# Kernel with wavelet, sparse attention and full attention, eight images, one core: the lone second attention of the last image gets instruction lists of its own

## The reference, cut to what matters

```
q = Wq x + bq ; k = Wk x + bk ; v = Wv x + bv          # 16 rows for q and k, 128 for v
attn = softmax(q^T k * 0.25, over the 4096 keys)
out  = gamma * (Wo (v attn^T) + bo) + x
```

## Time and profile before

| What | us |
|---|---|
| Three runs | 6031.35, 6034.84, 6043.09 |
| Their median | 6034.84 |
| The profiled execution: its span (the profile gives no other time for it) | 6037.8 |
| Last image's lone second attention, first matmul to end of span | 5557.97 to 6037.8, so 479.8 |

### The profile page before, as it was taken

One profiled execution on the slowest core, in us unless ns is written; L12 is line 12 of the kernel. 1 busy time (PEld: TensorE's weight loads), 2 busy tenths in 40 slices (PEclk: granted clock), 3 DMA queues, 4 the chain that ended last, 5 costly groups with the idle time before them and its releaser, 6 DMA issues.

```text
span 6037.8 us, 91146 instructions
## 1 busy us (share of the span) xinstructions
PE 4861.0 (81%) x30180; PEld 3018.9 (50%) x30180; DVE 4690.6 (78%) x8351; ACT 4552.4 (75%) x6907; POOL 429.0 (7%) x133
## 2 busy tenths in 40 slices
PE   4344788887988888887888878887888878886888
PEld 2000356553666446553556546553565535662666
DVE  3777699977998689977899778986898869984443
ACT  2995699948998589957999489966999589983223
POOL 3001200030000300021000300012000300000000
PEclk7555799997999889997999979998999979997999
DMA  1001200012001200012000120012000120011000
GB/s 64 6 10 48 69 14 15 14 53 71 19 15 50 72 16 15 16 55 69 16 15 20 62 58 15 17 56 70 14 15 14 52 71 19 14 36 39 9 11 10
DMA packets 104798, 199.90 MB, mean 33 GB/s; under 512 B 36632, under 2 KB 41656, under 8 KB 100184
## 3 DMA queue, kind: packets, MB, share of 16 engines
q1 hardware_dynamic: 104280, 193.56, 10.4%
HBM read 110.61 MB, written 82.05 MB: 32 GB/s over the span
## 4 chain that ended last, share of the span: by engine, by line
DVE 31%; PE 22%; issue 21%; ACT 18%; POOL 3%; SPq 2%; DMA 2%; DVEq 1%; ACTq 0%; POOLq 0%
ACT work L981 11%; DVE MX L1587 8%; PE PS L540 6%; DVE M L1438 6%; DVE arena L1516 5%; DVE work L1430 3%; PE PS L506 3%; DVE work L1422 3%; DVE work L1398 3%; ACT work L997 3%; POOL RN L2188 3%; ACT work L1004 2%; PE PS L859 2%; PE PS L844 2%; PE PS L756 2%
## 5 line engine op out<-in xcount | busy, mean ns | idle before, releaser
L981 ACT ACTIVATE work<-arena,T 128x1024 bf16<-128x1024 f32 x1792 | 2039.6, 1140 | 75.2 <-DVE T L1385 48.3
L540 PEld LDWEIGHTS PS<-V,work 128*128 128x128 f32 x16384 | 2010.1, 194 | 122.4 <-issue 29.5
L540 PE MATMUL PS<-V,work 128*128 128x129 f32 x16384 | 2040.3, 278 | 22.6 <-ACT work L1004 22.6
L1587 DVE TENSOR_REDUCE MX<-PS 128x1 f32<-128x512 f32 x2048 | 1395.1, 685 | 421.4 <-PE PS L506 403.9
L1004 ACT ACTIVATE work<-PS 128x1024 f32<-128x1024 f32 x1024 | 1040.4, 1016 | 410.9 <-PE PS L524 408.7
L506 PE MATMUL PS<-KP,QP 96*128 96x512 bf16 x2048 | 850.6, 417 | 352.7 <-DVE MX L1587 312.7
L1516 DVE SCALAR_TENSOR_TENSOR arena<-PS,work 128x1024 f32<-128x1024 f32 x512 | 622.5, 1216 | 100.7 <-ACT work L997 99.2
L524 PE MATMUL PS<-QP,KP 99*128 99x512 bf16 x2048 | 621.3, 385 | 69.3 <-ACT work L1004 38.4
L506 PEld LDWEIGHTS PS<-KP,QP 96*128 96x128 bf16 x2048 | 200.6, 98 | 924.2 <-DVE MX L1587 836.0
L997 ACT ACTIVATE work<-PS 128x1024 f32<-128x1024 f32 x512 | 520.3, 1016 | 142.9 <-PE PS L476 142.6
L1438 DVE MAX8 M<-work 128x8 f32<-128x1024 f32 x512 | 623.9, 1220 | 3.3
(11 more groups left out here) (180 smaller groups left out, 3994.4 us busy)
## 6 DMA issues: line engine op xcount, KB each, us to landing
scr<-work SPq DMA_DIRECT2D x96, 256.0 KB
work<-scr SPq DMA_DIRECT2D x128, 192.0 KB, 2.7
work<-in_x SPq DMA_DIRECT2D x16, 1024.0 KB, 7.7
arena<-in_x SPq DMA_DIRECT2D x8, 2048.0 KB, 11.3
scrX<-arena SPq DMA_DIRECT2D x8, 2048.0 KB, 14.1
XR<-scrX SPq DMA_DIRECT2D x64, 256.0 KB, 2.8
out<-YO SPq DMA_DIRECT2D x64, 256.0 KB, 2.1
scrL<-work SPq DMA_DIRECT2D x24, 512.0 KB, 14.8
```

Of the source, the lines that this page charges most:

```text
L540: last = mm(PS[:, 5 + i // 2, 136 * (i % 2):136 * (i % 2) + 129], P1[:, (16 * j + k) % 3, t, 128 * i:128 * i + 128], V1[:, mt, :], start=( ...
L981: A(JKA[:, m % 2, :], scores(h, i), ACT.Sign, scale=-1.0, bias=T[:, h % 2, i:i + 1], accum_out=CA[:, h % 2, i:i + 1]).then_inc(s["ca"], 1)
L1587: V.reduce_max(MX[:, c % 2, i, w:w + 1], PS[:, maxbank(c, k), :], AX.X).then_inc(s["mr"], 1)
```

## The change

Only the call `slots(8, False, True)` gets other instructions. All new banks and waits hang on `both` or `l0`, which is true in the merged stages.

- PSUM: maxima alternate between banks 4 and 7. The pairs of transposed scores alternate between 2, 3 and 0, 1.
- Waits: `maxima(c, k)` waits for the reduce before the last one, `l1_score` for the exponential before the last one. `maxima(c, 0)` waits for one output less. `l1_turn(j)` waits for one MPT more.
- Lists: PE, ACT, DVE and SP walk a list of their own. On PE, scores run up to two steps ahead of the weighing, three maxima lie around the halves of each weigh for k = 1 to 10, and `l1_turn(j - 1)` moves to just before the weigh 14 of chunk j. The first score of chunk j + 1 is put ahead of weigh 15 of chunk j.

```
-        def maxbank(c, k):
+        def maxbank(c, k, both):
+            if not both:
+                return 4 if k % 2 == 0 else 7
             return 6 if c == 0 and k % 2 else 4
+
+        def pairbanks(k, both):
+            return 2 if both or k % 2 == 0 else 0
...
@@ SP, slots
+                if l1 and not l0:
+                    for j in range(-1, NCH + 1):
+                        if chunk(j):
+                            load_rows(a, j)
+                        if chunk(j + 1):
+                            max_rows(a, j + 1)
+                        if chunk(j - 1):
+                            store(a, j - 1)
+                    return
...
@@ PE, maxima
-                    pe.wait_ge(s["mr"], a * 256 + c * 32 + k + (0 if c == 0 and k else 1))
+                    if l0:
+                        pe.wait_ge(s["mr"], a * 256 + c * 32 + k + (0 if c == 0 and k else 1))
+                    elif c or k:
+                        pe.wait_ge(s["mr"], a * 256 + c * 32 + k)
+                    else:
+                        pe.wait_ge(s["mr"], a * 256 + 1)
...
-                        pe.wait_ge(s["y1"], a * NCH + c + 1)
+                        pe.wait_ge(s["y1"], a * NCH + c + (1 if l0 else 0))
...
@@ PE, l1_score
-                    pe.wait_ge(s["e1"], a * 128 + j * 16 + k + 1)
+                    pe.wait_ge(s["e1"], a * 128 + j * 16 + k + (1 if l0 or (j == 0 and k == 0) else 0))
...
-                        last = mm(PS[:, 2 + t, :], KP1[0:KA, 128 * mt:128 * mt + 128], QP1[0:KA, j * 512:j * 512 + 512],
+                        last = mm(PS[:, pairbanks(k, l0) + t, :], KP1[0:KA, 128 * mt:128 * mt + 128], QP1[0:KA, j * 512:j * 512 + 512],
...
@@ PE, l1_weigh(j, k, halves=(0, 1)): one half is 8 of the 16 instructions
-                    for t in range(2):
+                    for t in halves:
...
-                    last.then_inc(s["pv1"], 1)
+                    if halves[-1] == 1:
+                        last.then_inc(s["pv1"], 1)
...
@@ PE, l1_turn
-                    pe.wait_ge(s["mpt"], a * NCH + min(j + 1, NCH - 1) + 2)
+                    pe.wait_ge(s["mpt"], a * NCH + min(j + (1 if l0 else 2), NCH - 1) + 2)
...
+                def chunks():                                  # PE
+                    for j in range(-1, NCH):
+                        l1_score(j, 1)
+                        maxima(j + 1, 0)
+                        maxima(j + 1, 1)
+                        for k in range(14):
+                            if k + 2 < 16:
+                                l1_score(j, k + 2)
+                            if 1 <= k < 11:
+                                maxima(j + 1, 3 * k - 1)
+                            l1_weigh(j, k, (0,))
+                            if 1 <= k < 11:
+                                maxima(j + 1, 3 * k)
+                            l1_weigh(j, k, (1,))
+                            if 1 <= k < 11:
+                                maxima(j + 1, 3 * k + 1)
+                            if k == 12:
+                                maxrow(j + 1)
+                        l1_turn(j - 1)
+                        l1_weigh(j, 14)
+                        l1_score(j + 1, 0)
+                        l1_weigh(j, 15)
...
+                if not l0:
+                    chunks()
+                    l1_turn(NCH - 1)
                     return
...
@@ ACT, l1_exp
-                    A(P1[:, (16 * j + k) % 3, :, :].rearrange("p t n -> p (t n)"), PS[:, 2:4, :].rearrange("p a n -> p (a n)"),
+                    u = pairbanks(k, l0)
+                    A(P1[:, (16 * j + k) % 3, :, :].rearrange("p t n -> p (t n)"), PS[:, u:u + 2, :].rearrange("p a n -> p (a n)"),
...
+                def chunks():                                  # ACT
+                    for j in range(-1, NCH):
+                        for k in range(14):
+                            l1_exp(j, k)
+                        maxrow(j + 1)
+                        l1_exp(j, 14)
+                        l1_exp(j, 15)
...
+                def chunks():                                  # DVE
+                    for j in range(-1, NCH):
+                        l1_norm(j - 1)
+                        maxima(j + 1, 0)
+                        maxima(j + 1, 1)
+                        for k in range(2, 32):
+                            maxima(j + 1, k)
+                        parts(j + 1)
+                        l1_out(j - 1)
+                    l1_norm(NCH - 1)
+                    l1_out(NCH - 1)
```

More of the change, by code:

```diff
@@ L505, in maxima @@
                     i, w = divmod(k, 8)
-                    mm(PS[:, maxbank(c, k), :], QP1[0:KS, c * 512 + 128 * i:c * 512 + 128 * i + 128], KP1[0:KS, 512 * w:512 * w + 512],
+                    mm(PS[:, maxbank(c, k, l0), :], QP1[0:KS, c * 512 + 128 * i:c * 512 + 128 * i + 128], KP1[0:KS, 512 * w:512 * w + 512],
                        start=True, stop=True).then_inc(s["m"], 1)
@@ L520, in l1_score, with l1_weigh @@
                         pe.wait_ge(s["mq"], a * (NCH * 48) + j * 48 + 96)
-                    pe.wait_ge(s["e1"], a * 128 + j * 16 + k + 1)
+                    pe.wait_ge(s["e1"], a * 128 + j * 16 + k + (1 if l0 or (j == 0 and k == 0) else 0))
                     for t in range(2):
                         mt = 2 * k + t
-                        last = mm(PS[:, 2 + t, :], KP1[0:KA, 128 * mt:128 * mt + 128], QP1[0:KA, j * 512:j * 512 + 512],
+                        last = mm(PS[:, pairbanks(k, l0) + t, :], KP1[0:KA, 128 * mt:128 * mt + 128], QP1[0:KA, j * 512:j * 512 + 512],
                                   start=True, stop=True)
                     last.then_inc(s["st1"], 1)
-                def l1_weigh(j, k):
+                def l1_weigh(j, k, halves=(0, 1)):
                     if not chunk(j):
@@ L677, in alone @@
                         score_t(h + 1, 3)
+                def chunks():
[20 more added lines that the diff above has]
+                        l1_weigh(j, 15)
                 if not l1:
                     alone()
+                    return
+                if not l0:
+                    chunks()
+                    l1_turn(NCH - 1)
                     return
@@ L1586, in maxima @@
                     dve.wait_ge(s["m"], a * 256 + c * 32 + k + 1)
-                    V.reduce_max(MX[:, c % 2, i, w:w + 1], PS[:, maxbank(c, k), :], AX.X).then_inc(s["mr"], 1)
+                    V.reduce_max(MX[:, c % 2, i, w:w + 1], PS[:, maxbank(c, k, l0), :], AX.X).then_inc(s["mr"], 1)
                 def parts(c):
@@ L1817, in alone @@
                         count(h + 1, 2, 7)
-                if l1:
+                def chunks():
[9 more added lines that the diff above has]
+                    l1_out(NCH - 1)
+                if l1 and not l0:
+                    chunks()
+                elif l1:
                     for h in range(-1, NH + 1):
```

## The result

| | before | after |
|---|---|---|
| Median of the runs, us | 6033.1 (4 runs, 6030.0 to 6043.1) | 5931.43 (4 runs, 5928.1 to 5939.3) |
| Ratio | | 0.9832, 95% interval 0.9818 to 0.9846 |
| Profiled span, us | 6037.8 | 5928.3 |
| Lone stage, first maxima matmul to end of span | 479.8 | 5549.04 to 5928.3, so 379.3 |
| Chunk 0, from its first score to its norm | 56.2 | 45.3 |

The kernel is 101.7 us faster (1.7%), against 100 forecast. The stage alone gives 100.5 in the two profiles: 6 x 13.80 + 10.9 + 6.8. The other 8.9 us between the two spans lie ahead of the stage, where no instruction was changed. The first maxima matmul of the stage stands at 5557.97 before and at 5549.04 after.

The account below looks back on a forecast made before the run. PE's work plus waits behind one maxima bank and at chunk ends bound the stage; savings of 83 (chunks 1 to 6), 9.8 (chunk 0) and 6.8 us (last), off median 6034.84, gave 5935 us, range 5924 to 5953.

Parts of the forecast that it names:

- A step: PE's score and weigh take 2.22 us, 16 times a chunk; the ten steps with three maxima matmuls take 2.88.
- The switch cost: Switching PE between bf16 and fp32 around weigh halves: taken as 0; exposed weight loads could cost 14 us in 7 chunks.
- A chunk: Norm to norm, chunks 1 to 6: 44.0 us against 57.81, saving 83 us over six.
- The stall at its end: PE's stall during the norm at a chunk's end: 0.3 us instead of 1.5, possibly between 0 and 1.5.
- Chunk 0: First score to last weigh issued: 42.7 us plus 3.5 for the lower clock, 46.2 against 56.0; saved 9.8.
- Last chunk: Norm to norm without maxima: 35.5 + 1.0 + 0.3 = 36.8 us against 43.6; saved 6.8.
- The range: 5924 to 5953 us: unknown costs from -3 to about +14 or +9, run spread -3.5 to +8.
- The clock: PE's granted clock after chunk ends: no more falls expected with the stall cut from 1.5 to 0.3 us.
- 1 (two banks as one): Maxima banks behave as one, three-maxima steps take at least 3.5 us instead of 2.88: 5979 us, chance 0.08.
- 2: Next chunk's first score gets its rows late, or the norm's cover fails: 25 us in seven chunks, 5960, chance 0.06.
- rival 3: PE's clock stays at or swings to the lower level in the new order: 6277 us if throughout, chance 0.03.
- 4: The new list makes no difference, the stage being bound by something the trace doesn't show: 6035 us, chance 0.01.

Follow-up runs that it names:

- e1: Changed kernel with one maxima bank and the wait for the reduce just before, score pairs staying two: 51.08 us a chunk, ratio to before 0.9961.
- e4: Changed kernel's new banks and waits, but the old merged lists on all engines: 46.92 us a chunk, ratio to before 0.9876.
- e3: Changed kernel with the turn back at the chunk's end, output right behind the norm, old waits: 45.91 us a chunk, one 47.54, ratio to before 0.9856.
- e6: Changed kernel with two maxima, then an undivided weigh, then the third maximum: 46.76 us a chunk, ratio to before 0.9869.
- the repeat: The changed kernel run again with nothing altered, beside the other experiments: 44.01 us a chunk, median 5936.73 us, ratio to before 0.9833.
- e2: Changed kernel with one score pair and the wait for the exponential just before, two maxima banks staying: 45.84 us a chunk, ratio to before 0.9862.
- e5: Changed kernel with PE's row of maxima (maxrow) one step later, behind weigh 13 instead of 12: 44.60 us a chunk, ratio to before 0.9845.
- e7: Changed kernel's new lists, but one maxima bank, one score pair and the stricter waits: 52.41 us a chunk, ratio to before 0.9970.

## Why the prediction was right

- **What bounds the stage.** PE's work plus waits behind one maxima bank: e1 and e4 show it from both sides. Of the 13.8 us a chunk, the banks give 10.9 on the old lists (57.81 to 46.92) and 8.4 on the new ones (52.41 to 44.01). The lists give 2.9 on the new banks and 5.4 on the old ones. The kernel before is the only one of the four whose clock fell behind chunk ends, and that is 1.2 us of its 57.81 (last section). Waits alone, the banks give 9.7 on the old lists, and the lists 4.2 on the old banks. Of the lists' 2.9, 1.9 is the turn's new place (e3); the other 1.0 I haven't taken apart.
- **A step.** 2.88 and 2.22 were forecast and measured. The switch cost, taken as 0 with 14 us kept in the range, is 0: the halves of a weigh take no longer than the whole (e6).
- **A chunk.** 44.0 forecast, 44.01 measured, six times over in each profile. The stall at its end was put at 0.3 and is 0.28.
- **Chunk 0.** 46.2 to the last weigh issued, measured about 45.1 (5576.49 to 5621.56), and 46.5 in the repeat. Two terms were off, one each way. The change puts chunk 1's first score ahead of chunk 0's weigh 15, and the sum left out its 0.43. And the loss to the clock was put at 3.5, with 7 us at the lower level, as before. In the profile after, the full level was back 3.8 us after the first score, in this window (columns as in the earlier trace rows):

```profile
5580.00:5581.00 1.00, 1.00 (x10) 1.00 (x9) 0.14 (x1) 0.87 (x1) 0.00 (x0) 0.84 0.00 0
```

That is a loss of 1.9, and 42.7 + 0.4 + 1.9 is the 45.1. In the repeat the same list got its clock back after 6.8 us (its first weigh prints 3.60 us, in the profile after 2.16). So the list alone doesn't set the moment, and the better part of the 1.1 us gained on the forecast is chance.
- **Last chunk.** 36.8 both, but this is in part luck: two errors cancel. The sum has 16 score pairs, while the chunk's first one is issued in chunk 6, 0.43 too much. And it has 0.3 of stall, while no maxima lie beside this norm:

```profile
5885.64 1.03 PE L543 MATMUL PS<-QP,KP 99*128 99x512 bf16 x4
5887.22 2.02 PE L559 MATMUL PS<-V,work 128*128 128x129 f32 x16 [0.55 <-DVE ON L1668]
```

Four matmuls are issued by about 5886.50, which leaves 0.72 of stall.
- **The median.** 5935 against 5931.4. The profiled span of before is 4.7 us over the median of its four runs, that of after 3.1 under its own. The sum was made of differences inside the stage, which this doesn't touch. The interval of the ratio leaves 93 to 110 us of gain, so that the medians come out at 101.7 against 100 is closer than the times can show. The rows of the stage carry the account.
- **The range.** It held, but its low end doesn't follow from its terms: 5935 - 3 - 3.5 is 5928.5, not 5924.
- **The second score pair** has no term of its own in my sum. e2 gives its price, on the new lists: 1.8 us a chunk, from two places in it.
- **The clock.** I wrote that with the stall at the chunk's end gone the falls would go. They did, yet e4 shows that the reason was at most half: it kept these stalls whole, and its clock didn't fall either.

The rivals: 1 (two banks as one) is what e1 does on purpose, and the change doesn't. 2 is out by e5. 3 is out: the granted clock was at its upper level from chunk 0's second weigh to the end. 4 is out by the time. The Trainium skill's rule in "TensorE: Matmul & The Clock Gate", section "A second HAM failure mode: psum-queue depth-cycling", would have given rival 3. It speaks of PE idle for moments between groups, and in this trace six banks are cycled through with PE busy 99.7%, so the moments are missing and the rule isn't put to the test. Where they are there, in e1 and e7, the clock stood at 1.00 behind chunk 0 all the same (windows in the last section).

## What to carry to other kernels

Where one engine fills a bank and another empties it, measure the ring (here matmul, reduce, wake-up: 1.17 us) and compare it with the spacing of those matmuls in the list. A second bank pays where the spacing is shorter, and two banks need the matmuls spread evenly (e6). Once the waits can go, forecast from the busiest engine's issue times, start to start, taken from a stretch without waits: that sum was right to 0.1 us in 44 for the six middle chunks. The first and the last chunk need counts of their own, of what the new order moves into them or out. A list written for merged stages is worth rewriting for the stage where it runs alone, but the banks it left for its partner are worth more.

## What the runs showed of the hardware that I hadn't expected

PE's clock fell after 5 of 7 chunk ends before (3.4 or 6.8 us at the lower level each), after one of 7 in e3, and after none in e4. Yet all three have the same idle time there, 1.3 + 0.5 us by the brackets. What differs is how busy PE was around it. The windows from the first to the seventh end, of the kernel before, e4 and e3, in that order:

```profile
5642.00:5988.00 346.00, 289.54 (x1972) 222.11 (x1973) 149.03 (x251) 99.92 (x102) 0.00 (x0) 0.98 0.03 10
5634.00:5915.00 281.00, 267.90 (x1974) 220.66 (x1974) 143.14 (x251) 99.98 (x102) 0.00 (x0) 1.00 0.04 12
5631.00:5908.00 277.00, 266.01 (x1975) 227.80 (x1974) 146.73 (x252) 98.48 (x102) 0.00 (x0) 0.99 0.04 12
```

PE was busy 83.7, 95.3 and 96.0% of these. So a short stall is not by itself what costs the clock; in the kernel before, more waits for the reduce followed it, and each step had its 0.52. e1 and e7, in that order, have waits in each step too, and one of 1.28 us at each chunk's end, and are busy 91.3 and 89.1%:

```profile
5663.00:5969.00 306.00, 279.34 (x1971) 221.12 (x1971) 148.81 (x252) 98.42 (x102) 0.00 (x0) 1.00 0.03 11
5658.00:5972.00 314.00, 279.76 (x1972) 221.17 (x1971) 148.76 (x252) 99.11 (x102) 0.00 (x0) 1.00 0.03 11
```

Their clock didn't fall once. So neither the waits in the steps (e1, e7) nor the old chunk ends (e4) brought the falls alone, but for one in e3; the kernel before has both. Each kernel stands on one or two profiles, and whether the place of the stall or the sum of waits decides stays open. The falls cost the kernel before about 1.2 us a chunk (57.81 on average, 56.63 in a chunk without one). With about 3.4 in its last chunk (half of 6.8 us at the lower level, an estimate) that is some 10 of the 100 us gained. The rest is waits, but for up to 1.6 by which chunk 0's clock came back sooner in the first profile.
